# Suffix sums in narrow steps of their own group, shift rows through VectorE and DRAM, operand loads behind them

## The chip, the cores and the metric

One core of one Trainium2 chip. The metric is the device time of one execution in microseconds; a kernel's time is the median of its runs.

## The reference, cut to what matters

```python
x, shape (2, 2048, 256), all float32
xn = layernorm(x)
q, k, v = split(xn @ w_in.T)              # 16 heads of 16
att = (q @ k.T) / 4                       # per head, 2048 x 2048
att = where(causal, att, 0.0)             # a masked score is 0, not -inf
out = softmax(att) @ v                    # so masked keys keep a weight exp(0 - max)
y = x + out @ w_out.T + sigmoid(xr @ W_r.T) * (relu(xk @ W_k.T)**2 @ W_v.T)
# xr, xk: xn mixed with the token before it by mu_r, mu_k
```

Because masked scores are zero, each query needs, besides its causal keys, the plain sum of the values of all later keys: the suffix sum, weighted by exp(-max). And the row maximum of each query has to be known before the exponentials.

## The kernel before

**Token stage** (to about 228 us). Eight chunks of 512 tokens are normalised, projected to q, k, v, run through the feed-forward part and stored in DRAM: q and k as a high and a low part in `parts_d`, v in `vpad_d`.

**Attention stage.** Eight groups of four heads, G = 0 to 7. G is 2i + p, and p (0 or 1) says which half of the double buffers `q_op`, `k_op`, `v_sb`, `v_after` it uses. A group has four units u = 0 to 3 of 512 queries; unit u has 4(u+1) key tiles, so that a group has 40 steps, numbered 0 to 39 here: unit 0 is steps 0 to 3, unit 1 steps 4 to 11, unit 2 steps 12 to 23, unit 3 steps 24 to 39. A step (u, kt) is written out by hand on TensorE: four score matmuls (L1175, one for each head, in two pairs), in between two "pieces" of the row maxima (L330, L337: the scores once more, turned, for VectorE to reduce at L347), then what `between_scores` adds, then `weigh_values` (L1189) of the step two before. The last four key tiles of a unit are on the diagonal and 512, 384, 256 and 128 queries wide; these narrow steps have less score work.

**Row maxima run ahead.** The 80 pieces of a group do not stand in its own steps. From step 17 on (`AHEAD_FROM`, L44) the pieces are those of the next group, 46 of them, and steps 0 to 16 hold the other 34 of the group itself. So piece 0 of the next group, in step 17, is the first thing that reads that group's `q_op` and `k_op`, and TensorE waits for their loads there (L1259 to L1261).

**Shift rows.** When a unit's pieces are reduced, three small VectorE instructions (`max_step`, L349: L355, L359, L362) make its negated maximum in two parts, `shift`, [128 queries, 4 blocks x 8 values]. It is turned by four TensorE transposes into a bank of `ps_s` (`turn_shift`, L1149, L1154), copied by ScalarE (`keep_shift`, L1014, L1019) to `shift_t` [8, 512], and stored by four SP DMAs in rows of `q_op` (`place_shift`, L300, L306), so that the score matmul subtracts it. This stands at `SHIFT_AT` (L55): units 0 and 1 of the next group in steps (3, 3) and (3, 10), unit 2 in (1, 2), unit 3 in (2, 8). Two units are turned in the token stage (`TOKEN_SHIFT_AT`, L52; L744, L667).

**Suffix sums.** GpSimd adds up the values behind each tile (`add_up_after`, L313, L320) in `after`; for each of four quads of tiles TensorE adds two matmuls (`sum_suffix`, L1158: L1164, L1165), and ScalarE copies them to `v_after` (L1011). They are made for the next group, in steps (3, 2), (3, 4), (3, 7), (3, 9) of unit 3 (`SV_AT`, L56); group 0 makes its own in steps (0, 0) to (0, 3). `masked_keys` (L1194) uses them in the second step of the unit behind.

**The ring.** Scores, suffix sums and turned shifts share three banks of `ps_s`; each use waits for ScalarE's reading of the use three before (`wait_for_bank`, L1132), and ScalarE reads in the same order.

**The SP queue** (`group`, L891) is one list of waits and DMAs in order. In a group: wait for the end of the scores of the group before; load the next group's `q_op` and `k_op` (`load_scores`, L275: 12 DMAs of 256 KB); store the normalised output of unit 3 of the group before (`keep_normed`, L879, L884: 4 DMAs, behind a wait for VectorE's L1091); `place_shift` of unit 2; load the next values (L311, 1 MB); the outputs of units 0 and 1; `place_shift` of unit 3; the output of unit 2; `place_shift` of the next group's units 0 and 1. TensorE waits for a unit's shift rows at its first step (L1252).

Of the kernel before, what the change touches and what calls it, by code (L numbers as in the profile page):

```python
# [22 lines left out]
GH = 4  # L23
# [87 lines left out]
def score_uses(first, last):  # L111

    uses = []
    for u in range(NCH):
        for kt in range(key_tiles(u)):
            uses += [("scores", (KT0[u] + kt) * GH + at) for at in range(GH // 2)]
            if first and (u, kt) in FIRST_SV_AT:
                uses.append(("own suffix", FIRST_SV_AT[u, kt]))
            if (u, kt) in SV_AT and not last:
                uses.append(("suffix", SV_AT[u, kt]))  # L120
            if (u, kt) in SHIFT_AT and not (u == NCH - 1 and last):
                uses.append(("shift", SHIFT_AT[u, kt]))
# [72 lines left out]
class Operands:  # L195
# [3 lines left out]
    def __init__(self, nc, ctx, parts_d, vpad_d):  # L199
# [10 lines left out]
        self.after = sb("after", [P, NT, GH, HD])  # L210
# [8 lines left out]
        self.shift_t = sb("shift_t", [SHIFT_PARTS * GH, 2, CH])  # L219
# [12 lines left out]
        self.shift_turned, self.shift_t_ready = sem("shift_turned"), sem("shift_t_ready")  # L232
        self.shift_loaded = [sem("shift_loaded0"), sem("shift_loaded1")]
        self.SHIFTS = SHIFT_PARTS * 2 * 16
        self.parts_in = parts_d.rearrange("r (z b) (cc g e j d) t -> r z (b cc) g e d j t", b=B, cc=CC, g=2, e=2, j=GH // 2)
        self.v_in = vpad_d.rearrange("(i g) p t f -> i g p t f", g=2)

    def set_constants(self, pool):
# [4 lines left out]
        pool.memset(self.after[:, NT - 1], 0.0).then_inc(self.consts_set, 1)  # L243
# [69 lines left out]
    def add_up_after(self, pool, p, n, loads):  # L313
# [3 lines left out]
        for j in range(NT - 2, -1, -1):  # L317
            if j < NT - 2:
                pool.wait_ge(self.after_ready, n * (NT - 1) + NT - 2 - j)
            pool.tensor_tensor(self.after[:, j], self.after[:, j + 1], values[:, j + 1, :, 0:HD], ALU.add).then_inc(self.after_ready, 1)  # L320
# [28 lines left out]
    def max_step(self, dve, k, u, n, reduced):  # L349
# [27 lines left out]
def stage_tokens(nc, block, x, w_in_t, w_r_t, w_k_t, w_v_t, w_out_t, mu_rk,  # L377
                 parts_d, vpad_d, ffn_d, ident, w_out_sb, consts_ready, ops, stores):

    with ExitStack() as ctx:  # L380
# [259 lines left out]
        def _(act):  # L640
# [23 lines left out]
            def keep_shift(u):  # L664

                act.wait_ge(ops.shift_turned, u + 1)
                act.copy(ops.shift_t[:, u], ps_m[0:SHIFT_PARTS * GH, 0]).then_inc(ops.shift_t_ready, 1)  # L667

            def batch(b, last):
                for c in range(NCH):  # L670
# [6 lines left out]
                    if (n, 0) in TOKEN_SHIFT_AT:  # L677
                        keep_shift(TOKEN_SHIFT_AT[n, 0])
# [10 lines left out]
                    if (n, 6) in TOKEN_SHIFT_AT:  # L689
                        keep_shift(TOKEN_SHIFT_AT[n, 6])  # L690
# [14 lines left out]
        def _(pe):  # L705
# [31 lines left out]
            piece_behind_turn = {pieces_beside_tokens(*at).stop: u for at, u in TOKEN_SHIFT_AT.items()}  # L737

            def turn_shift(u, pieces_before):

                pe.wait_ge(ops.shift_ready, u + 1)
                pe.wait_ge(ops.piece_reduced, pieces_before + MRING)
                for s in range(SUB):
                    last = pe.transpose(ps_m[0:SHIFT_PARTS * GH, 0, s * P:(s + 1) * P],  # L744
                                        ops.shift[:, u, s].rearrange("p r h -> p (r h)"), ident[:])
# [573 lines left out]
```

## Time and profile before

| | us |
|---|---|
| median of 3 runs (lowest, highest) | 1128.43 (1125.78, 1129.91) |
| the profiled execution's own time | 1134.35 |
| its span | 1132.6 |
| TensorE busy | 1080.0 (95%) |
| VectorE busy | 842.5 (74%) |
| ScalarE busy | 713.4 (63%) |
| GpSimd busy | 385.8 (34%) |
| mean granted clock of TensorE | 0.983 |

The profile is one execution, recorded by the hardware. A busy TensorE is one that has some matmul under way, which isn't a TensorE at its peak: matmuls are pipelined, and pairs of them run side by side. SPq is the SP engine's DMA queue; the time beside a DMA there is that of its issue, not of its transfer. "Issue" as a releaser is a wait for nothing that the profile shows. The clock column gives 1.00 for 2.4 GHz and 0.50 for 1.2 GHz.

### The profile page before, as it was taken

The page shows a single profiled execution, that of the slowest core. Times are in us where ns is not written, and L with a number is a line of the kernel's source. Part 1 is how long each engine was busy: PE and PEld are TensorE (multiplying, and loading weights), DVE is VectorE, ACT ScalarE, POOL GpSimd, SP SyncE. Part 2 cuts the span into 40 slices and gives each one's busy share as a digit, 9 for nine tenths or more (in the row PEclk, how much of TensorE's full clock was granted, in tenths as well). Part 3 has the DMA queues.
Part 4 walks back from the last instruction along what each step waited for, and adds up shares of the span by engine and source line. Part 5 has one row for each costly group of instructions (what it writes and reads, how often), then busy time and mean ns, then how long its engine had stood idle before and what let it go on. Part 6 is the DMA issues. An engine that isn't in the chain of part 4 may idle for free.

```text
span 1132.6 us, 21906 instructions
## 1 busy us (share of the span) xinstructions
PE 1080.0 (95%) x8192; PEld 542.6 (48%) x8192; DVE 842.5 (74%) x1153; ACT 713.4 (63%) x1519; POOL 385.8 (34%) x945
## 2 busy tenths in 40 slices
PE   5999998999999999999989999999999989999998
PEld 3665554544444444444435444444444434444445
DVE  5567787678879787987867878878887878789213
ACT  2433333267776677777757776777777657767672
POOL 3211121354414341444224424442532433244301
PEclk9999999999999899999969999999999989999999
DMA  3585744392019000900280019002800460002033
GB/s 127 174 271 177 214 149 149 131 117 62 2 20 122 30 3 17 124 31 7 37 119 11 6 22 140 8 7 38 124 6 6 58 104 7 6 2 86 25 98 117
DMA packets 53390, 83.61 MB, mean 74 GB/s; under 512 B 6308, under 2 KB 36260, under 8 KB 49572
## 3 DMA queue, kind: packets, MB, share of 16 engines
q1 hardware_dynamic: 52132, 78.01, 32.9%
q0 software_dynamic: 1152, 4.19, 1.2%
q8 instruction: 65, 1.06, 0.4%
q14 instruction: 41, 0.34, 0.1%
HBM read 43.78 MB, written 33.55 MB: 68 GB/s over the span
## 4 chain that ended last, share of the span: by engine, by line
PE 75%; DVE 13%; ACT 4%; issue 4%; DMA 2%; POOL 0%; SPq 0%; ACTq 0%; DVEq 0%; POOLq 0%
PE ps_o L1189 22%; PE ps_s L1175 21%; DVE part_max L347 10%; PE ps_m L330 7%; PE ps_vr L733 4%; ACT probs L1039 4%; PE ps_qk L724 4%; PE ps_m L1220 3%; PE ps_o L1200 2%; PE ps_m L337 2%; PE ps_xt L782 2%; PE ps_qk L733 2%; PE ps_s L1164 2%; DMA x_in<-x 1%; PE ps_pieces L330 1%
## 5 line engine op out<-in xcount | busy, mean ns | idle before, releaser
L1039 ACT ACTIVATE probs<-ps_s 128x512 f32<-128x512 f32 (+3 forms) x1280 | 599.6, 536 | 249.6 <-PE ps_s L1175 241.5
L347 DVE TENSOR_REDUCE part_max<-ps_m 128x2 f32<-128x1024 f32 (+2 forms) x594 | 616.6, 1059 | 152.7 <-PE ps_m L330 115.1
L1175 PE MATMUL ps_s<-q_op,k_op 50*128 50x512 f32 (+3 forms) x1280 | 447.9, 429 | 10.0 <-ACT probs L1039 5.2
L330 PE MATMUL ps_m<-k_op,q_op 48*128 48x512 f32 (+3 forms) x1188 | 355.3, 419 | 16.6 <-DVE part_max L347 9.4
L1175 PEld LDWEIGHTS ps_s<-q_op,k_op 50*128 50x128 f32 x1280 | 210.7, 188 | 313.1 <-ACT probs L1039 214.2
L984 POOL TENSOR_SCALAR_AFFINE_SELECT probs<-probs 128x128 f32<-128x128 f32 x512 | 145.0, 292 | 485.7 <-ACT probs L1039 477.2
L1189 PE MATMUL ps_o<-probs,v_sb 128*32 128x512 f32 (+3 forms) x2560 | 307.9, 551 | 2.2 <-issue 2.2
L330 PEld LDWEIGHTS ps_m<-k_op,q_op 48*128 48x128 f32 x1188 | 169.3, 189 | 43.8 <-DVE part_max L347 33.8
L950 POOL TENSOR_TENSOR diag_weight<-ident,masked_weight 128x256 f32<-128x256 f32 x256 | 150.5, 623 | 40.7 <-ACT masked_weight L1005 40.7
L337 PE MATMUL ps_m<-mask,pick 64*128 64x64 bf16 (+1 forms) x932 | 96.5, 210 | 0.0
L1189 PEld LDWEIGHTS ps_o<-probs,v_sb 128*32 128x32 f32 x2560 | 51.1, 108 | 76.7 <-issue 38.1
L347 DVE TENSOR_REDUCE part_max<-ps_pieces 128x2 f32<-128x1024 f32 (+3 forms) x46 | 46.5, 1011 | 35.2 <-PE ps_pieces L337 18.4
L724 PE MATMUL ps_qk<-xn_t,w_in_sb 128*128 128x512 f32 x128 | 63.2, 624 | 1.9 <-issue 1.4
L656 ACT ACTIVATE parts<-ps_qk 128x512 fp32r<-128x512 f32 x32 | 19.1, 597 | 71.2 <-PE ps_qk L724 71.2
L516 POOL TENSOR_TENSOR k_act<-k_act 128x1024 f32<-128x1024 f32 x8 | 15.3, 1909 | 122.4 <-ACT k_act L688 122.4
L337 PEld LDWEIGHTS ps_m<-mask,pick 64*128 64x128 bf16 x932 | 46.6, 97 | 9.9 <-issue 2.5
L320 POOL TENSOR_TENSOR after<-after,v_sb 128x64 f32<-128x64 f32 x120 | 39.5, 329 | 8.8
L521 POOL TENSOR_TENSOR ffn<-ffn,x_in 128x512 f32<-128x512 f32 x16 | 21.4, 1345 | 51.4 <-DVE ffn L589 51.4
L724 PEld LDWEIGHTS ps_qk<-xn_t,w_in_sb 128*128 128x128 f32 x128 | 23.5, 196 | 25.2 <-issue 24.1
L1200 PE MATMUL ps_o<-diag_weight,v_after 128*32 128x128 f32 x1024 | 35.2, 279 | 0.0
L1220 PE MATMUL ps_m<-w_out_sb,attn_t 128*128 128x256 f32 x128 | 33.3, 397 | 0.0
L1200 PEld LDWEIGHTS ps_o<-diag_weight,v_after 128*32 128x32 f32 x1024 | 26.7, 111 | 11.6 <-POOL diag_weight L950 8.0
(81 smaller groups left out, 715.9 us busy)
## 6 DMA issues: line engine op xcount, KB each, us to landing
parts_d<-parts SPq DMA_DIRECT2D x32, 512.0 KB, 4.7
q_op<-parts_d SPq DMA_DIRECT2D x42, 256.0 KB, 13.9
k_op<-parts_d SPq DMA_DIRECT2D x42, 256.0 KB, 16.2
vpad_d<-v_pad SPq DMA_DIRECT2D x32, 256.0 KB, 3.3
v_sb<-vpad_d SPq DMA_DIRECT2D x8, 1024.0 KB, 12.4
x_in<-x SPq DMA_DIRECT2D x8, 512.0 KB, 5.2
ffn_d<-ffn SPq DMA_DIRECT2D x8, 512.0 KB, 3.2
attn_t<-normed SPq DMA_DIRECT2D x128, 32.0 KB, 2.0
```

The source lines that it names most:

```text
L330: last = pe.matmul(ps_m[:, f % ring * 2 + e, 0:width], self.q_op[rows, p, j, q0:q0 + P], self.k_op[rows, p, j, pc * CH:pc * CH + width], s ...
L337: last = pe.matmul(ps_m[:, f % ring * 2 + e, s * P + k * HALF:width], self.pick16[half, k], self.mask16[half, k, k * HALF:P], start=False, ...
L347: dve.tensor_reduce(both, ps_m[:, bank:bank + 2, 0:width], AX_X, ALU.max).then_inc(self.piece_reduced, 1)
L724: last = pe.matmul(ps_qk[:, j % 2], w_in_sb[:, cc, j * P:(j + 1) * P], xn_t[:, cc, 1:CH + 1], start=(cc == 0), stop=(cc == CC - 1))
L733: last = pe.matmul(psum[:, s], lhs[:, cc, t * P:(t + 1) * P], weights[:, cc], start=(cc == 0), stop=(cc == CC - 1))
L950: pool.tensor_tensor(diag_weight[:, u % 2, some], ident[:].unsqueeze(1).broadcast_to([P, GH * SUB // DIAGS, P]), masked_weight[:, u, some] ...
L984: pool.affine_select(out=blk, in_=blk, compare_op=ALU.is_ge, fill=0.0, base=0, pattern=[[1, P]], channel_multiplier=-1).then_inc(probs_mas ...
L1039: act.activation(probs[:, slot % PRING, 0:width], ps_s[:, bank_of("scores", slot, first, last), 0:width], ACT.Exp).then_inc(probs_ready, 1)
L1175: pe.matmul(ps_s[:, bank_of("scores", slot, first, last), 0:CH - q0], k_op[rows, p, h % 2, kt * P:(kt + 1) * P], q_op[rows, p, h % 2, u * ...
L1189: last = pe.matmul(ps_o[h * HW:(h + 1) * HW, q0:CH], v_sb[:, p, kt, h * HW:(h + 1) * HW], probs[:, ((KT0[u] + kt) * GH + at) % PRING, 0:CH ...
L1200: last = pe.matmul(ps_o[h * HW:(h + 1) * HW, s * P:(s + 1) * P], v_after[:, p, u * SUB + s, h * HW:(h + 1) * HW], diag_weight[:, u % 2, h ...
L1220: last = pe.matmul(ps_m[:, k % MBANKS, 0:C], attn_t[:, b * CC + cc, c * CH + t * P:c * CH + (t + 1) * P], w_out_sb[:, cc], start=(cc == 0) ...
```

## The change

The suffix sums of a group are made in that group itself, in its steps (0, 2), (0, 3), (1, 6) and (2, 10), and `after` becomes a double buffer, so that GpSimd no longer waits for its readers. The shift is no longer turned on TensorE: a fourth `max_step` on VectorE transposes [128, 32] in blocks of 32 x 32, SP stores the result in a DRAM tensor `shift_d` by four DMAs, waits until they have landed, and loads the rows of `q_op` from there by four DMAs. In the SP queue, `load_scores` stands behind `keep_normed` of unit 3 and `place_shift` of unit 2. The bank order of `ps_s` runs on through all groups.

```diff
-TOKEN_SHIFT_AT = {(6, 0): 0, (6, 6): 1}
-SHIFT_AT = {(3, 3): 0, (3, 10): 1, (1, 2): 2, (2, 8): 3}
-SV_AT = {(3, 2): 0, (3, 4): 1, (3, 7): 2, (3, 9): 3}
-FIRST_SV_AT = {(0, 0): 0, (0, 1): 1, (0, 2): 2, (0, 3): 3}
-MAX_STEPS = 3
+WEIGHT_AT = {(3, 3): 0, (3, 10): 1, (1, 2): 2, (2, 8): 3}
+SV_AT = {(0, 2): 0, (0, 3): 1, (1, 6): 2, (2, 10): 3}
+MAX_STEPS = 4
...
-def bank_of(what, which, first, last):
+def bank_of(what, which, G):
-    return (score_uses(first, last).index((what, which)) + 2 * first) % SRING
+    return (G * len(score_uses()) + score_uses().index((what, which))) % SRING
...
-        self.after = sb("after", [P, NT, GH, HD])
+        self.after = sb("after", [P, 2, NT, GH, HD])
-        self.shift_t = sb("shift_t", [SHIFT_PARTS * GH, 2, CH])
+        self.shift_t = sb("shift_t", [P, 2, HW])
+        self.shift_d = nc.dram_tensor("shift_d", [2, SHIFT_PARTS, 2, GH // 2, CH], F32, kind="Internal").ap()
...
     def place_shift(self, sp, p, u, n):
         sp.wait_ge(self.shift_t_ready, n + 1)
+        sp.wait_ge(self.shift_loaded[u % 2], (n // 2 + 1) * self.SHIFTS)
+        by_block = self.shift_d[u % 2].rearrange("r e j (s b w) -> b s (r e j) w", s=SUB, w=HW)
+        for b in range(P // HW):
+            sp.dma_start(by_block[b], self.shift_t[b * HW:(b + 1) * HW, u % 2]).then_inc(self.shift_stored, 16)
+        sp.wait_ge(self.shift_stored, (n + 1) * (P // HW) * 16)
         for part in range(SHIFT_PARTS):
             for e in range(2):
-                row, at = e * HALF + ROWS + part, part * GH + e * 2
+                row = e * HALF + ROWS + part
                 sp.dma_start(self.q_op[row:row + 1, p, :, u * CH:(u + 1) * CH].bitcast(F32),
-                             self.shift_t[at:at + 2, u % 2]).then_inc(self.shift_loaded[u % 2], 16)
+                             self.shift_d[u % 2, part, e].unsqueeze(0)).then_inc(self.shift_loaded[u % 2], 16)
...
+        if k == 3:
+            dve.wait_ge(self.shift_ready, n + 1)
+            if n >= 2:
+                dve.wait_ge(self.shift_stored, (n - 1) * (P // HW) * 16)
+            dve.transpose(self.shift_t[:, u % 2], self.shift[:, u].rearrange("p s r h -> p (s r h)")).then_inc(self.shift_t_ready, 1)
...
             def group(i, p, first=False, last=False):          # SP
-                if not last:
-                    if not first:
-                        sp.wait_ge(scores_ready, (i * 2 + p) * SLOTS)
-                    ops.load_scores(sp, i + p, 1 - p)
                 if not first:
                     keep_normed(i - 1 + p, 1 - p, NCH - 1)
                 ops.place_shift(sp, p, 2, unit_of(i, p, 2))
                 if not last:
+                    if not first:
+                        sp.wait_ge(scores_ready, (i * 2 + p) * SLOTS)
+                    ops.load_scores(sp, i + p, 1 - p)
                     sp.wait_ge(masked_done, unit_of(i, p, 0) + 1)
                     sp.wait_ge(probs_used, weighed_to(unit_of(i, p, 0)))
                     ops.load_values(sp, i + p, 1 - p)
...
                     if u == 2 and not last:                    # GpSimd
-                        pool.wait_ge(v_after_ready, G * 4 + 4)
                         ops.add_up_after(pool, 1 - p, G + 1, i + 1 + p)
...
             def masked_keys(p, u, G):                          # TensorE
                 pe.wait_ge(diag_ready, (G * NCH + u + 1) * DIAGS)
-                pe.wait_ge(v_after_ready, G * 4 + 4)
+                pe.wait_ge(v_after_ready, G * 4 + u + 1)
...
-                if (u, kt) in SV_AT and not last:
-                    wait_for_bank("suffix", SV_AT[u, kt], i, p, first, last)
-                    sum_suffix(1 - p, SV_AT[u, kt], G + 1, bank_of("suffix", SV_AT[u, kt], first, last))
-                if (u, kt) in SHIFT_AT and not (nxt and last):
-                    v = SHIFT_AT[u, kt]
-                    wait_for_bank("shift", v, i, p, first, last)
-                    turn_shift(v, unit_of(i, p, v + nxt), bank_of("shift", v, first, last))
+                if (u, kt) in SV_AT:
+                    wait_for_bank("suffix", SV_AT[u, kt], i, p, first)
+                    sum_suffix(p, SV_AT[u, kt], G, bank_of("suffix", SV_AT[u, kt], G))
```

Both `turn_shift` and both `keep_shift` functions, of the token and of the attention stage, go with their calls and their bank uses; `weight` (L1002) stays at the places in `WEIGHT_AT`.

## Rows read from the trace of the kernel before

**Rows 1.** The page: busy time, share of the span and instructions.

```profile
PE 1080.0 (95%) x8192; PEld 542.6 (48%) x8192; DVE 842.5 (74%) x1153; ACT 713.4 (63%) x1519; POOL 385.8 (34%) x945
```

**Rows 2.** TensorE's instructions in time, group 5: start us, us, engine, line.

```profile
785.10 0.50 PE L1175 MATMUL ps_s<-q_op,k_op 50*128 50x512 f32 x1
...
829.54 0.32 PE L330 MATMUL ps_m<-k_op,q_op 48*128 48x128 f32 x1
...
837.54 0.50 PE L1175 MATMUL ps_s<-q_op,k_op 50*128 50x512 f32 x1
...
840.72 0.44 PE L1175 MATMUL ps_s<-q_op,k_op 50*128 50x384 f32 x1
...
871.53 0.50 PE L1175 MATMUL ps_s<-q_op,k_op 50*128 50x512 f32 x1
...
874.20 0.50 PE L1175 MATMUL ps_s<-q_op,k_op 50*128 50x512 f32 x1
...
877.72 0.49 PE L1175 MATMUL ps_s<-q_op,k_op 50*128 50x512 f32 x1
```

**Rows 3.** The SP queue in time, groups 5 and 6: start us, us of issue.

```profile
784.42 0.31 SPq L280 DMA_DIRECT2D q_op<-parts_d  x1
...
789.44 0.42 SPq L282 DMA_DIRECT2D k_op<-parts_d  x1
799.62 3.75 SPq L884 DMA_DIRECT2D attn_t<-normed  x4
803.42 2.46 SPq L306 DMA_DIRECT2D q_op<-shift_t  x4
...
907.79 2.48 SPq L884 DMA_DIRECT2D attn_t<-normed  x4
```

**Rows 4.** DMA issues in 789.4 to 789.9 us: KB, us to landing.

```profile
k_op<-parts_d SPq DMA_DIRECT2D x1, 256.0 KB, 24.7
```

**Rows 5.** DMA issues in 832.3 to 832.6 us.

```profile
attn_t<-normed SPq DMA_DIRECT2D x2, 32.0 KB, 1.9
```

**Rows 6.** Stretches: us, busy of the engines, clock, DMA share, GB/s.

```profile
676.10:688.00 11.90, 11.35 (x130) 5.83 (x126) 11.68 (x17) 8.53 (x21) 7.17 (x22) 1.00 1.04 126
...
829.50:893.30 63.80, 62.93 (x526) 30.17 (x522) 48.99 (x61) 46.69 (x104) 18.44 (x48) 1.00 0.03 6
```

**Rows 7.** The same view around the longest idle stretches of TensorE.

```profile
573.00:576.00 3.00, 0.20 (x2) 0.20 (x2) 0.23 (x1) 0.43 (x1) 0.00 (x0) 0.95 1.07 117
576.00:597.00 21.00, 21.00 (x106) 9.31 (x106) 13.48 (x15) 11.55 (x24) 3.35 (x12) 0.52 0.68 114
...
903.00:910.00 7.00, 4.00 (x57) 1.99 (x53) 4.69 (x6) 3.80 (x7) 4.43 (x8) 1.00 1.04 117
910.00:917.00 7.00, 6.83 (x35) 2.84 (x35) 4.03 (x4) 4.14 (x8) 0.00 (x0) 0.51 1.03 118
```

**Rows 8.** The SP queue, the same store in groups 1, 3, 4 and 7.

```profile
352.60 2.47 SPq L884 DMA_DIRECT2D attn_t<-normed  x4
...
573.26 2.46 SPq L884 DMA_DIRECT2D attn_t<-normed  x4
...
690.60 2.45 SPq L884 DMA_DIRECT2D attn_t<-normed  x4
...
1021.23 2.45 SPq L884 DMA_DIRECT2D attn_t<-normed  x4
```

**Rows 9.** Groups of instructions: count, busy us, mean ns, idle before.

```profile
L320 POOL TENSOR_TENSOR after<-after,v_sb 128x64 f32<-128x64 f32 x120 | 39.5, 329 | 8.8
...
L1091 DVE STREAM_TRANSPOSE normed<-turned 128x512 f32<-128x512 f32 x32 | 22.4, 701 | 0.0
...
L362 DVE SCALAR_TENSOR_TENSOR shift<-row_max,shift 128x16 f32<-128x16 f32 x32 | 5.9, 185 | 0.3
```

**Rows 10.** TensorE in time in the token stage, around its two turned shifts.

```profile
175.40 0.44 PE L330 MATMUL ps_pieces<-k_op,q_op 48*128 48x384 f32 x2 [1.14 <-ACT shift_t L667]
...
191.50 0.49 PE L330 MATMUL ps_pieces<-k_op,q_op 48*128 48x512 f32 x2 [1.57 <-ACT shift_t L667]
```

More of the change, by code:

```diff
@@ L108, in pieces_at, with score_uses @@
     return SPREAD[u, kt, half], KT0[u] + kt >= AHEAD_FROM
-def score_uses(first, last):
+def score_uses():
     uses = []
@@ L735, in two_tiles @@
                 return last
[L737 to L745, printed above, removed]
-                last.then_inc(ops.shift_turned, 1)
             def batch(b, last_batch):
@@ L1039, in group @@
                             act.activation(probs[:, slot % PRING, 0:width],
-                                           ps_s[:, bank_of("scores", slot, first, last), 0:width], ACT.Exp).then_inc(probs_ready, 1)
+                                           ps_s[:, bank_of("scores", slot, i * 2 + p), 0:width], ACT.Exp).then_inc(probs_ready, 1)
                             if h != GH // 2 - 1:
                                 continue
-                            if first and (u, kt) in FIRST_SV_AT:
-                                keep_suffix(0, FIRST_SV_AT[u, kt], FIRST_SV_AT[u, kt],
-                                            bank_of("own suffix", FIRST_SV_AT[u, kt], first, last))
-                            if (u, kt) in SV_AT and not last:
-                                keep_suffix(1 - p, SV_AT[u, kt], (G + 1) * 4 + SV_AT[u, kt],
-                                            bank_of("suffix", SV_AT[u, kt], first, last))
-                            if (u, kt) in SHIFT_AT and not (nxt and last):
-                                v = SHIFT_AT[u, kt]
-                                weight(unit_of(i, p, v + nxt), v)
-                                keep_shift(v, unit_of(i, p, v + nxt), (G + (nxt > 0)) * (NCH // 2) + v // 2,
-                                           bank_of("shift", v, first, last))
+                            if (u, kt) in SV_AT:
+                                keep_suffix(p, SV_AT[u, kt], G * 4 + SV_AT[u, kt], bank_of("suffix", SV_AT[u, kt], G))
+                            if (u, kt) in WEIGHT_AT and not (nxt and last):
+                                weight(unit_of(i, p, WEIGHT_AT[u, kt] + nxt), WEIGHT_AT[u, kt])
                         if kt == LAG - 1 and not (first and u == 0):
@@ L1131, in _, with wait_for_bank @@
         def _(pe):
-            def wait_for_bank(what, which, i, p, first, last):
-                uses = score_uses(first, last)
+            def wait_for_bank(what, which, i, p, first):
+                uses = score_uses()
                 G = i * 2 + p
@@ L1141, in wait_for_bank @@
                     pe.wait_ge(probs_ready, G * SLOTS + uses[at][1] + 1 + SRING)
-                elif uses[at][0] == "own suffix":
-                    pe.wait_ge(v_after_ready, uses[at][1] + 1)
-                elif uses[at][0] == "suffix":
-                    pe.wait_ge(v_after_ready, (G + 1) * 4 + uses[at][1] + 1)
-                else:
-                    pe.wait_ge(shift_t_ready, unit_of(i, p, uses[at][1] + (NCH if uses[at][1] < 2 else 0)) + 1)
-            def turn_shift(u, n, bank):
-                pe.wait_ge(shift_ready, n + 1)
-                for s in range(SUB):
-                    last = pe.transpose(ps_s[0:SHIFT_PARTS * GH, bank, s * P:(s + 1) * P],
-                                        shift[:, u, s].rearrange("p r h -> p (r h)"), ident[:])
-                last.then_inc(shift_turned, 1)
+                else:
+                    pe.wait_ge(v_after_ready, G * 4 + uses[at][1] + 1)
             def sum_suffix(p, quad, n, bank):
@@ L1164, in sum_suffix @@
                 pe.matmul(ps_s[:, bank, 0:width], keys_after[:], values, start=True, stop=False)
-                pe.matmul(ps_s[:, bank, 0:width], ones[:], after[:, tiles].rearrange("p s h d -> p (s h d)"),
+                pe.matmul(ps_s[:, bank, 0:width], ones[:], after[:, p, tiles].rearrange("p s h d -> p (s h d)"),
                           start=False, stop=True).then_inc(suffix_ready, 1)
@@ L1173, in score_tile @@
                 q0 = first_query(u, kt)
-                wait_for_bank("scores", slot, i, p, first, last)
-                pe.matmul(ps_s[:, bank_of("scores", slot, first, last), 0:CH - q0], k_op[rows, p, h % 2, kt * P:(kt + 1) * P],
+                wait_for_bank("scores", slot, i, p, first)
+                pe.matmul(ps_s[:, bank_of("scores", slot, i * 2 + p), 0:CH - q0], k_op[rows, p, h % 2, kt * P:(kt + 1) * P],
                           q_op[rows, p, h % 2, u * CH + q0:(u + 1) * CH], start=True, stop=True).then_inc(scores_ready, 1)
@@ L1233, in between_scores @@
                     output_tile(OUT_AT[u, kt])
[L1234 to L1243 removed]
+                if (u, kt) in SV_AT:
+                    wait_for_bank("suffix", SV_AT[u, kt], i, p, first)
+                    sum_suffix(p, SV_AT[u, kt], G, bank_of("suffix", SV_AT[u, kt], G))
             def group(i, p, first=False, last=False):
```

38 lines of the change are left out of this document (6 added, 32 removed).

## The prediction

> **What bounds the kernel now.** I read the page first: TensorE is busy 95% of the span [rows 1]. The chain of waits and the SP queue's own view come next, since this change touches TensorE's list, VectorE's list and the order of the SP queue. From step 12 on a group is TensorE's: in the stretch from step 17 to the end of group 5 it is busy 62.93 of 63.80 us with VectorE at 48.99 (the second of [rows 6]), and a plain step of unit 3 takes 874.20 - 871.53 = 2.67 us, start to start [rows 2]. Steps 0 to 4 are VectorE's: 11.68 busy of 11.90 us, TensorE 11.35 (the first of [rows 6]). Then the loads: the twelve DMAs of the next group's scores are issued from 784.42 on, 0.7 us before the group's first matmul at 785.10 [rows 2, 3], and the last, issued at 789.44, lands 24.7 us later, at 814.1 [rows 3, 4]. That is 29.7 us for 3 MB, with the DMA engines full (share 1.04 in the first stretch of [rows 6]). The first reader, piece 0 of the next group, starts at 829.54 [rows 2]. So the loads have 15.4 us of slack. That slack is what the change spends.
>
> **The start of the loads.** New order in the SP queue: output of unit 3, shift of unit 2, then the loads. The output waits for VectorE and is issued 799.62 - 785.10 = 14.5 us into the group. Behind it: four issues, 2.5 us (3.75 here); four stores of the shift, of which the last is issued 1.85 us after the first (three quarters of 2.46 for four issues [rows 3]) and lands some 1.9 us later [rows 5]; four loads of the rows, 2.5 us; with 0.4 us between them 9.2 us in all. The loads start at 14.5 + 9.2 = 23.7 us of the group instead of -0.7, and land 30 us later, at 53.7.
>
> The output itself comes later by x: two suffix sums (0.85 each on TensorE, below) and VectorE's fourth step stand ahead of it in steps 2 and 3. Nothing of it shows if VectorE hides it (TensorE is idle 0.55 of 11.90 us there), 1.9 if nothing hides it. I take x = 0.9, the middle, since the rows show both engines nearly full.
>
> **When they are wanted.** Step 17 starts 829.54 - 785.10 = 44.4 us into the group. It loses one turned shift (-0.5), gains x and y, the suffix sum in (1, 6), which costs 0 to 0.85; I take 0.5. That is 44.4 - 0.5 + 0.9 + 0.5 = 45.3. The loads land at 53.7 + 0.9 = 54.6. **TensorE stands still for 9.3 us in step 17 of groups 1 to 6.** Groups 1 to 6 alone: group 7 has no loads, and in group 0 SP waits for no output, only for the maximum of unit 2 in step 2, so its loads start at about 9 + 6.6 us (an estimate: the time of four steps, then stores, wait and loads), land at 46 and cost 0 to 1 us.
>
> **What the stall costs behind it.** The trace has two such gaps, both shorter. TensorE is busy 0.20 us from 573 to 576, and the granted clock is 0.52 for the 21 us behind it, which is 1.2 GHz. In 903 to 910 it is idle 3.0 us, and the clock is 0.51 for the next 7 us [rows 7]. From output to output those groups take 690.60 - 573.26 = 117.3 and 1021.23 - 907.79 = 113.4 us, against 907.79 - 799.62 = 108.2 for group 5 [rows 3, 8]. Less the gap (2.8 and 3.0) the low clock costs 6.3 and 2.2 us. I take C = 3.8 for each stall, nearer to the middle than to an end, as nothing says which it will be.
>
> The Trainium skill (TensorE: Matmul & The Clock Gate, HAM oscillation) tells of a matmul kernel that waits for DMA once in each iteration and runs the start of every iteration at the low clock. By it C is paid in all six groups. The sum above takes C six times as well; only if a gap left the clock alone would it be less.
>
> **What the change saves.** A turned shift costs 840.72 - 837.54 = 3.18 us for its step, against 2.67: 0.5 us, four in a group. A suffix sum in unit 3 costs 877.72 - 874.20 = 3.52, so 0.85 [rows 2]. Of the four in unit 3 I count 3.05: three at 0.85 and 0.5 for the one in (3, 2), where ScalarE's copy of the unit before comes between the scores and would hold the step up anyway. The same sums come back in narrow steps: x, y and 0.85 in (2, 10), where [rows 6] shows TensorE full. So narrow steps save little, because TensorE's own work for a sum is the same and only VectorE's steps 0 to 4 could hide it. ScalarE's copies go at no gain of their own: it was ahead.
>
> Added on VectorE: 32 transposes of 128 x 32. The trace has 128 x 512 at 0.70 us as the upper end, and the neighbour L362 on 128 x 16 at 0.19 as the lower [rows 9]; I take 0.2, as these short ones are all start-up. In steps 16, 22 and 30 TensorE covers it, which would cost 0.2 to 0.7 each uncovered; in step 2 it is in x. GpSimd's sums wait for the values, which now land at about 59 instead of 33 us of the group; its masks for step 20 then queue up to 5 us behind (15 sums of 0.33 [rows 9]), and their reader stands two steps later, so I cost it at 0, at most 2 us a group. The shift rows are wanted at 8 to 17 us after SP gets to them and take 7: cost 0, with up to 2 in unit 3, where they queue behind the values.
>
> **The sum.** The part behind step 17 was 108.2 - 44.4 = 63.8 us. It becomes 63.8 - 1.5 (three turned shifts) - 3.05 + 0.85 = 60.1. A group: 54.6 + 60.1 + 3.8 = 118.5. Six of them: 711.0, against 1021.23 - 352.60 = 668.6 before [rows 8]: +42.4. (In those 668.6 stand the two stalls above and smaller ones, all ahead of step 17 while the loads run. They are paid for already now: whatever is lost ahead of step 17 is taken out of the wait there.) Group 0: four turned shifts and the later sums, -2.0 - 3.05 with its own four sums only moved, +0.5 of wait: -4.5. Group 7: it had no sums and two turned shifts: +0.9 + 0.5 + 0.85 - 1.0 = +1.3. Token stage: two turned shifts with the gaps of 1.14 and 1.57 us behind them [rows 10] and 0.5 each: between 0 and -4; -3. Sum: 42.4 - 4.5 + 1.3 - 3.0 = +36.2 on the profiled execution's 1134.35, that is 1170.5. The median of the runs shown is 1128.43, 5.9 lower; stalls ahead of step 17 that vary from run to run would be absorbed in the new kernel, so I take off only 2.5 of it: **1168 us**, 3.5% slower.
>
> **The rivals.**
>
> *The loads land in time (faster).* Point of decision: they must take 45.3 - 24.6 = 20.7 us or less where [rows 3, 4] show 29.7. For it: behind the shift they run beside other traffic, and no row shows them at another place. Against it: the engines' share is already 1.04 with nothing else in the queue but 128 KB of outputs. Then a group is worth 2.0 + 3.05 - 0.9 - 0.5 - 0.85 = 2.8 less, six groups -17, with group 0, 7 and the token stage -23: about 1110 from the profiled execution's time. The Trainium skill (DMA: Bandwidth & Descriptors, Measured) gives 6.15 us for 1 MB spread over 128 partitions, some 18 us for 3 MB as an estimate, and by it this rival would hold. These rows go to 16 partitions each, the trace has 29.7 us, and the measurement decides. Chance 0.08.
>
> *The loads are late by some 4 us (no change).* If they take 25 us, six stalls of 4 us with little low clock give back what the steps saved: about 1128. Chance 0.04.
>
> *The low clock lasts.* The stall is three times as long as the ones of the trace. If each costs the 6.3 us of group 3 or a little more, six times 2.5 to 4 is added: 1183 to 1192. Chance 0.15.
>
> *The change doesn't do what it says.* The first reader of the loads would have to stand later than step 17, so that no wait arises. `AHEAD_FROM` and L1259 are untouched; I see no way, and fold it into the first rival.
>
> The forecast itself has 0.73.
>
> **The range.** Its bounds are 29.7 or 31 us for the loads (-2 to +6 over six groups), C from 2.2 to 6.3 (-10 to +15), y (-3 to +2; x cancels in the stall but not in the arrival: -5 to +6), GpSimd and the shift of unit 3 (up to +10), token stage (-1 to +3), the distance to the median (-3.5 to +2.5). Together I give 1148 to 1189, which leaves out the first two rivals and the far end of the third. A measurement of this kernel tells 0.5% from no change. Faster by more: 0.08. Within: 0.04. Slower: 0.88.
>
> **What the new profile would show.** Right: in groups 1 to 6 a wait of about 9 us of TensorE at L330's weight load, released by a DMA into `q_op` or `k_op`, once a group; DMA-filled slices in the middle of a group; the clock at 0.5 behind each wait; plain steps of unit 3 at 2.67 with no 3.5 among them; six groups of 117 to 120 us; the first stalls for which nothing is shown gone from the sum. Wrong: loads that land within 21 us; a wait at step 17 under 5 us; an unmoved clock behind it (then -20 us); or shift rows that come late for unit 2 or 3, which would show as waits on `q_op<-shift_d` at L1175.

## The result, and the profile after

| | before | after |
|---|---|---|
| median (lowest, highest), 4 runs each on one chip, us | 1129.17 (1125.78, 1132.36) | 1181.68 (1178.22, 1184.88) |
| ratio, 95% interval | | 1.0465 (1.0415 to 1.0514) |
| the profiled execution's own time, its span, us | 1134.35, 1132.6 | 1184.88, 1182.8 |
| mean granted clock of TensorE | 0.983 | 0.942 |

The change makes the kernel 4.7% slower. I measured each group from its first score matmul to that of the next group, in us. These lengths are used all the way down:

| kernel | group 0 | groups 1 to 6 (sum) | group 7 to the end |
|---|---|---|---|
| before | 110.4 | 113.0, 107.7, 117.3, 109.0, 108.2, 113.5 (668.6) | 125.9 |
| after | 114.6 | 118.1, 118.5, 120.3, 119.5, 118.4, 120.3 (715.1) | 127.4 |

So the groups 1 to 6 take 46.5 us more, group 0 4.2 more, group 7 1.5 more; the first group starts 2.0 us earlier (225.64 against 227.65). Together 50.2, the difference of the spans.

The page of the kernel after: busy times, then the slices of TensorE, its clock and the DMA engines, then two groups of instructions (busy us, mean ns, idle before and its releaser):

```profile
PE 1091.6 (92%) x8064; PEld 550.5 (47%) x8064; DVE 847.0 (72%) x1185; ACT 699.6 (59%) x1487; POOL 386.0 (33%) x945
...
PE   5999999999999699969997999799969996999998
...
PEclk9999999879999799979996999699979996999999
DMA  4575644391006400640064006500550055002033
...
L330 PEld LDWEIGHTS ps_m<-k_op,q_op 48*128 48x128 f32 x1188 | 176.8, 196 | 88.5 <-issue 45.6
...
L320 POOL TENSOR_TENSOR after<-after,v_sb 128x64 f32<-128x64 f32 x120 | 39.4, 328 | 136.6 <-DMA v_sb<-vpad_d 127.9
```

Read the slices together. TensorE has a dent once in each of the groups 1 to 6, the dent follows on the fullest DMA slices, and the clock is down in the same slice. In slices 8 and 9 the clock is down without a dent: that is group 0. TensorE ran 128 fewer matmuls than in [rows 1] and was busy 11.6 us longer: part of its work ran at the low clock. GpSimd waited 127.9 us for the values, seven times, against 8.8 us of all idle time before [rows 9], and nobody was held up by it here.

The SP queue of group 5, whose first matmul starts at 816.66 (start, us of issue):

```profile
832.61 2.47 SPq L864 DMA_DIRECT2D attn_t<-normed  x4
835.18 2.60 SPq L301 DMA_DIRECT2D shift_d<-shift_t  x4
838.93 2.34 SPq L306 DMA_DIRECT2D q_op<-shift_d  x4
841.31 0.40 SPq L275 DMA_DIRECT2D q_op<-parts_d  x1
...
846.42 0.42 SPq L277 DMA_DIRECT2D k_op<-parts_d  x1
```

And the landing of the last of these loads (KB, us to landing):

```profile
k_op<-parts_d SPq DMA_DIRECT2D x1, 256.0 KB, 24.9
```

It answers to [rows 3, 4]: the output stands at +15.95 us of the group instead of +14.5, the loads start at +24.65 instead of -0.7, and the last lands at 846.42 + 24.9 = 871.3, or +54.7. They took 30.0 us, as before (29.7). TensorE at that time:

```profile
862.03 0.49 PE L1125 MATMUL ps_s<-q_op,k_op 50*128 50x512 f32 x1
...
871.45 0.47 PE L330 MATMUL ps_m<-k_op,q_op 48*128 48x128 f32 x2 [8.93 <-issue]
...
873.59 1.93 PE L1139 MATMUL ps_o<-probs,v_sb 128*32 128x512 f32 x8
```

Step 17 begins at +45.4, and piece 0 follows 9.4 us later, 0.1 us after the landing (9.0 to 9.6 us in the six groups, 9.3 in the mean). The idle time is put down to "issue", although what ended it is a load. The chain that ended last gives the load its place (start, us, what):

```profile
845.96 23.83 DMA q_op<-parts_d
869.79 1.67 issue
871.45 0.47 PE ps_m L330 x2
```

In the chain the load has its whole way of 23.83 us, where TensorE lost 9: on the page's chain that makes a share of 14% for DMA, though the six waits are 5% of the span. Last, the stretches around the wait (busy of PE, PEld, DVE, ACT, POOL; clock; DMA share; GB/s):

```profile
862.00:864.50 2.50, 0.52 (x5) 0.18 (x1) 1.64 (x5) 0.62 (x2) 0.00 (x0) 1.00 1.00 111
864.50:871.50 7.00, 0.05 (x2) 0.08 (x2) 0.00 (x0) 0.00 (x0) 0.00 (x0) 0.50 0.98 159
871.50:881.60 10.10, 10.10 (x62) 5.55 (x62) 4.29 (x6) 4.67 (x9) 4.78 (x15) 0.50 0.23 71
881.60:935.00 53.40, 52.37 (x436) 24.35 (x435) 43.09 (x53) 39.25 (x88) 18.41 (x48) 1.00 0.02 5
```

The clock falls to 1.2 GHz while TensorE waits and stays there for the first 10.1 us of work. Step 18 takes 4.45 us and step 19 3.02, where a plain one takes 2.67.

### The profile page after: what moved, and what is told of

Same layout as the page of the kernel before. It is cut to its first block, busy times and chain, and to the rows that moved or that the text cites. A ratio compares the mean times of both kernels' runs of the same rounds, so it can differ in the third digit from the quotient of the medians.

```text
span 1182.8 us, 21770 instructions
## 1 busy us (share of the span) xinstructions
PE 1091.6 (92%) x8064; PEld 550.5 (47%) x8064; DVE 847.0 (72%) x1185; ACT 699.6 (59%) x1487; POOL 386.0 (33%) x945
## 3 DMA queue, kind: packets, MB, share of 16 engines
q8 instruction: 63, 1.03, 0.4%
## 4 chain that ended last, share of the span: by engine, by line
PE 65%; DMA 14%; DVE 11%; issue 4%; ACT 3%; SPq 2%; POOL 0%; ACTq 0%; DVEq 0%; POOLq 0%
PE ps_o L1139 19%; PE ps_s L1125 17%; DMA q_op<-parts_d 12%; DVE part_max L347 7%; PE ps_m L330 7%; PE ps_vr L729 4%; ACT probs L1009 3%; PE ps_qk L720 3%; PE ps_m L1170 3%; PE ps_xt L763 2%; PE ps_m L337 2%; PE ps_qk L729 2%; PE ps_o L1150 2%; PE ps_s L1114 1%; DMA x_in<-x 1%
## 5 line engine op out<-in xcount | busy, mean ns | idle before, releaser
L1125 PE MATMUL ps_s<-q_op,k_op 50*128 50x512 f32 (+3 forms) x1280 | 457.7, 442 | 9.1 <-ACT probs L1009 5.2
L1125 PEld LDWEIGHTS ps_s<-q_op,k_op 50*128 50x128 f32 x1280 | 218.3, 194 | 320.5 <-ACT probs L1009 225.7
L1139 PE MATMUL ps_o<-probs,v_sb 128*32 128x512 f32 (+3 forms) x2560 | 315.8, 567 | 0.0
L330 PEld LDWEIGHTS ps_m<-k_op,q_op 48*128 48x128 f32 x1188 | 176.8, 196 | 88.5 <-issue 45.6
L337 PE MATMUL ps_m<-mask,pick 64*128 64x64 bf16 (+1 forms) x932 | 104.2, 223 | 0.0
L320 POOL TENSOR_TENSOR after<-after,v_sb 128x64 f32<-128x64 f32 x120 | 39.4, 328 | 136.6 <-DMA v_sb<-vpad_d 127.9
L337 PEld LDWEIGHTS ps_m<-mask,pick 64*128 64x128 bf16 x932 | 51.1, 104 | 16.0 <-issue 3.2
L720 PEld LDWEIGHTS ps_qk<-xn_t,w_in_sb 128*128 128x128 f32 x128 | 23.4, 195 | 25.4 <-issue 23.6
L1150 PEld LDWEIGHTS ps_o<-diag_weight,v_after 128*32 128x32 f32 x1024 | 26.7, 111 | 11.6 <-POOL diag_weight L928 6.2
```

The lines of the kernel that those rows point to most:

```text
L330: last = pe.matmul(ps_m[:, f % ring * 2 + e, 0:width], self.q_op[rows, p, j, q0:q0 + P], self.k_op[rows, p, j, pc * CH:pc * CH + width], s ...
L337: last = pe.matmul(ps_m[:, f % ring * 2 + e, s * P + k * HALF:width], self.pick16[half, k], self.mask16[half, k, k * HALF:P], start=False, ...
L720: last = pe.matmul(ps_qk[:, j % 2], w_in_sb[:, cc, j * P:(j + 1) * P], xn_t[:, cc, 1:CH + 1], start=(cc == 0), stop=(cc == CC - 1))
L1125: pe.matmul(ps_s[:, bank_of("scores", slot, i * 2 + p), 0:CH - q0], k_op[rows, p, h % 2, kt * P:(kt + 1) * P], q_op[rows, p, h % 2, u * CH ...
L1139: last = pe.matmul(ps_o[h * HW:(h + 1) * HW, q0:CH], v_sb[:, p, kt, h * HW:(h + 1) * HW], probs[:, ((KT0[u] + kt) * GH + at) % PRING, 0:CH ...
L1150: last = pe.matmul(ps_o[h * HW:(h + 1) * HW, s * P:(s + 1) * P], v_after[:, p, u * SUB + s, h * HW:(h + 1) * HW], diag_weight[:, u % 2, h ...
```

## The experiments

**Theory.** The loads start behind the output and the shift's two trips and land after step 17 has begun. Groups 1 to 6 each pay some 9.4 us of wait and some 4 us of low clock. **Rivals.** The shift's way through DRAM, its added transfers, or the suffix sums in narrow steps cost the time. And for group 0, which has no such wait of this length and yet is 4.2 us longer, something else must be found. Where nothing else is said, a kernel is the one after with the edit shown.

### Only the loads put back in front

```diff
             def group(i, p, first=False, last=False):          # SP
+                if not last:
+                    if not first:
+                        sp.wait_ge(scores_ready, (i * 2 + p) * SLOTS)
+                    ops.load_scores(sp, i + p, 1 - p)
                 if not first:
                     keep_normed(i - 1 + p, 1 - p, NCH - 1)
                 ops.place_shift(sp, p, 2, unit_of(i, p, 2))
                 if not last:
-                    if not first:
-                        sp.wait_ge(scores_ready, (i * 2 + p) * SLOTS)
-                    ops.load_scores(sp, i + p, 1 - p)
```

> The changed kernel with the twelve score loads put back in front of the output of unit 3 and the shift of unit 2. Theory (the time is lost at step 17, waiting for loads that start 24.7 us into the group): the wait of 9.3 us and the low clock behind it go, a group is 105.5 us (the clean steps of the changed kernel) plus a wait in step 12, because the shift rows of unit 2 now stand behind the loads twice: stored at about 30 us of the group, loaded at about 34.5 where step 12 starts at 31.5, so some 3 us; with stalls ahead of step 17 as in the kernel before (0 to 23 us in all) 1115 to 1140 us, ratio to before 0.99 to 1.01. Rival (the trip of the shift rows through DRAM is what costs, wherever the loads stand): stays above 1165 us, with waits for shift rows in every unit.

Measured: 1129.14 us, ratio 0.9972 (0.9943 to 1.0001). Groups 1 to 6 take 664.3. All the loss is gone, so what the change adds elsewhere doesn't cost it. But no gain is left either, and the rows of unit 2 now come late in step 12 (waited for: us in total, times, longest):

```profile
PEld ps_s L1126 <- DMA q_op<-shift_d: 11.6, 4, 3.2
...
PE ps_s L1126 <- DMA q_op<-shift_d: 8.8, 4, 2.5
```

With the loads in front of them, the shift's two trips run while the DMA engines are full: in groups 1 to 6 the last load of the rows is issued 11 to 12 us after the last of the stores, against 3.6 us in the kernel after. I expected such a wait of some 3 us in each group; it came in four of seven, and the other three lose their time elsewhere (last section).

### Shift, loads, output

```diff
             def group(i, p, first=False, last=False):          # SP
-                if not first:
-                    keep_normed(i - 1 + p, 1 - p, NCH - 1)
                 ops.place_shift(sp, p, 2, unit_of(i, p, 2))
                 if not last:
                     if not first:
                         sp.wait_ge(scores_ready, (i * 2 + p) * SLOTS)
                     ops.load_scores(sp, i + p, 1 - p)
+                if not first:
+                    keep_normed(i - 1 + p, 1 - p, NCH - 1)
```

> The changed kernel with the SP queue in the order shift of unit 2, score loads, output of unit 3. The shift is ready 6.9 us into the group and takes 6.2 us on SP, so the loads start at 13.3 and land at 43.4, ahead of step 17 at 45.4. Theory: no wait at step 17, a group of 105.5 us plus what the loads' own stalls cost (0 to 23 us over six groups): 1099 to 1124 us, ratio 0.975 to 0.995, faster than both. Rival (the low clock comes from the narrow steps or the DRAM trip and not from the wait): the clock still falls in each group, over 1150 us.

Measured: 1102.18 us, ratio 0.9713 (0.9664 to 0.9761). Groups 1 to 6 take 633.7, five of them 105.5 to 105.8. In group 5, which starts at 762.68:

```profile
773.53 2.33 SPq L306 DMA_DIRECT2D q_op<-shift_d  x4
775.91 0.40 SPq L275 DMA_DIRECT2D q_op<-parts_d  x1
...
781.48 2.47 SPq L864 DMA_DIRECT2D attn_t<-normed  x4
```

The loads start at +13.2 and have landed at +43.1; step 17 begins at +45.4, and nothing waits. The order of three entries in one queue is worth some 80 us; by the profiles it is 81.4 in groups 1 to 6. The time is in the expected range, the ratio a little below it. This kernel also gives the full price of a late group: (715.1 - 633.7) / 6 = 13.57 us, less 9.33 of wait in the mean, leaves 4.2 for what comes behind it. Group 0 stayed at 114.7, so its loss has another cause.

### The first reader three steps later

```diff
-AHEAD_FROM = 17
+AHEAD_FROM = 20
```

> The changed kernel with AHEAD_FROM 20 instead of 17: the loads stay where they are, their first reader moves three steps of 2.67 us later, to 53.4 us of the group, against 54.7 for the landing. Theory: a wait of 1.3 us in step 20 instead of 9.3 in step 17, too short for the clock: groups of 107 us, 1105 to 1120 us in all. Rival (the DMA traffic in the middle of the group slows the steps themselves): no better than 1165 us.

Measured: 1150.15 us, ratio 1.0145 (1.0083 to 1.0208): 31 us less than after, and at least 30 above what I expected. Groups 1 to 6 take 688.6. In step 20 the wait is 0 to 2.4 us (1.3 expected). A larger wait stands in step 22, which takes 3.22 us in the kernel after and 4.6 to 7.8 here: it is behind GpSimd. Group 5, GpSimd and then TensorE:

```profile
848.68 5.88 POOL L320 TENSOR_TENSOR after<-after,v_sb 128x64 f32<-128x64 f32 x15 [18.92 <-DMA v_sb<-vpad_d]
854.51 2.98 POOL L961 TENSOR_SCALAR_AFFINE_SELECT probs<-probs 128x128 f32<-128x128 f32 x12
```

```profile
855.60 1.06 PE L1139 MATMUL ps_o<-probs,v_sb 128*32 128x512 f32 x4 [1.51 <-POOL probs L961]
```

GpSimd stands before its suffix sums until the values, the last of the loads, have landed; twelve masks of unit 2's diagonal queue up behind, and their reader waits for them. In the kernel after, the wait in step 17 held TensorE back by more than that, so nothing showed.

### The same, with GpSimd's sums a unit later

```diff
-AHEAD_FROM = 17
+AHEAD_FROM = 20
...
-                    if u == 2 and not last:                    # GpSimd
+                    if u == 3 and not last:
                         ops.add_up_after(pool, 1 - p, G + 1, i + 1 + p)
```

> The kernel with AHEAD_FROM 20 (1150 us, with waits of 2.4 to 4.6 us in step 22 that nobody foresaw), and GpSimd's adding up of the values moved from the start of unit 2 to the start of unit 3 in its list. Theory (GpSimd waits for the values, which land behind the scores at 59 us of the group, and its masks for steps 20 and 21 are queued behind the sums): the wait in step 22 goes, groups of 106 to 108 us, 1100 to 1112 us in all. Rival (the DMA traffic at that time or the narrow steps themselves are slow): step 22 keeps its wait, 1145 us or more.

Measured: 1126.31 us, ratio 0.995 (0.9918 to 0.9982), groups 1 to 6 657.1. Step 22 takes 3.23 us in every group instead of 4.6 to 7.8: GpSimd was the cause. The size is missed by some 14 us. The profiled execution took 1115.26 us, 11 less than the median, so its groups show less than the usual loss. What is left in it against the 633.7 of the order above: waits of up to 2.4 us in step 20, and steps 2 to 8, which are longer with the pieces at other places, with low clock in steps 6 to 8 of three groups and behind the wait in two.

### The kernel before, with only the SP queue's new order

```diff
             def group(i, p, first=False, last=False):          # SP, before.py
-                if not last:
-                    if not first:
-                        sp.wait_ge(scores_ready, (i * 2 + p) * SLOTS)
-                    ops.load_scores(sp, i + p, 1 - p)
                 if not first:
                     keep_normed(i - 1 + p, 1 - p, NCH - 1)
                 ops.place_shift(sp, p, 2, unit_of(i, p, 2))
+                if not last:
+                    if not first:
+                        sp.wait_ge(scores_ready, (i * 2 + p) * SLOTS)
+                    ops.load_scores(sp, i + p, 1 - p)
```

> The kernel before with one part of the change alone: the loads behind the output of unit 3 and the shift of unit 2. They start 14.5 + 2.7 + 2.6 = 19.8 us into the group and land at 49.8; step 17 stands at 44.4. Theory: a wait of 5.4 us and 2 to 4 us of low clock in six groups, a group of 116.3 us, less the stalls ahead of step 17, which the wait absorbs: 1150 to 1168 us, ratio 1.02 to 1.035. Rival (the order of the loads alone does nothing, the narrow steps and the DRAM trip do it): within 0.5% of before.

Measured: 1183.33 us, ratio 1.0441 (1.0397 to 1.0485). The groups 1 to 6 take 701.6. Without one transpose on VectorE or one sum moved, the reordering alone costs as much as the whole change does. That the totals are so near is chance, since the parts differ. Groups 1 to 6 lose 33.0 us here and 46.5 with the whole change: the loads start at +19.7 instead of +24.65, and the wait is 4.6 to 5.8 us instead of 9.3. Group 0 loses 13.0 us here and 4.2 there, and it is why the total is above what I expected. It takes 123.4 us against 110.4: its loads stand behind the shift of unit 2, which TensorE turns only in step 6. They start 22.1 us into the group, TensorE waits 5.8 us in step 17, and the clock stays low for 23.9 us.

```profile
248.31 2.39 SPq L306 DMA_DIRECT2D q_op<-shift_t  x4
250.74 0.40 SPq L280 DMA_DIRECT2D q_op<-parts_d  x1
```

### TensorE kept busy in the wait

Nine dummy matmuls (128 x 512, the identity by `w_out_sb`, into a bank of `ps_m` that is overwritten next; the trace lists two rows for each) stand in front of the wait, in group 0 too, which has none. No work is left out.

```diff
                                     if ahead and f == 0:
+                                        pe.wait_ge(ops.piece_reduced, (G + ahead) * PIECES + 1)
+                                        for _ in range(WARM):
+                                            pe.matmul(ps_m[:, 0], ident[:], w_out_sb[:].rearrange("p a c -> p (a c)"),
+                                                      start=True, stop=True)
                                         pe.wait_ge(q_loaded[1 - p], ops.loaded(1 - p, i + 1 + p))
```

> The changed kernel, with nine matmuls of 128 x 512 (0.94 us each at the full clock, 8.5 us, by the projections of the token stage) put ahead of the wait in step 17, written to a bank that piece 0 then overwrites. They do no work; they only fill the 9.3 us of the wait. Theory (13 us lost a group are 9.3 of waiting and the rest of low clock behind it): the wait stays, the clock stays at 2.4 GHz, and six groups win 3 to 5 us each: 1150 to 1165 us. Rival A (all the loss is waiting, the low clock only shows it): same as the changed kernel, 1182. Rival B (nine matmuls more are work more): slower than 1182 by up to 50 us.

Measured: 1159.72 us, ratio 1.0248 (1.0211 to 1.0286). Groups 1 to 6 take 689.1, 25.9 less than after. The loads are as late as they were, and piece 0 starts 8.8 to 9.8 us behind its step; what differs is the clock. Group 5:

```profile
847.61 7.99 PE L1206 MATMUL ps_m<-w_out_sb,ident 128*128 128x512 f32 x18
856.60 0.33 PE L331 MATMUL ps_m<-k_op,q_op 48*128 48x128 f32 x2 [0.99 <-issue]
```

```profile
849.00:858.70 9.70, 8.71 (x39) 3.65 (x37) 1.62 (x3) 1.35 (x3) 0.00 (x0) 1.00 0.90 176
```

The gain is 25.9 / 6 = 4.3 us a wait, but the clock held in five groups only. In group 4, where TensorE idled 1.33 us behind the dummies (1.18 at most in the others), it fell for 6.8 us, and the group took 117.3 us. The other five, at 114.1 to 114.7, are 4.8 us shorter in the mean than in the kernel after. That agrees with the 4.2 from above: with the clock kept, these five groups are 8.7 us longer than without a wait, though piece 0 starts 9.2 us late, so that 0.4 us of a wait is won back and the low clock itself has to cost some 4.7.

### Where the suffix sums stand

Three kernels, each on the order "shift, loads, output". In the first the sums of steps (0, 2) and (0, 3) go to the two steps ahead of them:

```diff
-SV_AT = {(0, 2): 0, (0, 3): 1, (1, 6): 2, (2, 10): 3}
+SV_AT = {(0, 0): 0, (0, 1): 1, (1, 6): 2, (2, 10): 3}
```

> The kernel with the SP order shift, loads, output (1102 us), and the first two suffix sums in steps (0, 0) and (0, 1) instead of (0, 2) and (0, 3). Theory (in group 0 the sums of the kernel before filled the gaps of TensorE in the first two steps of the attention stage, and without them the clock falls for 24 us and costs some 8 us): group 0 keeps its clock and is 8 us shorter, other groups within 1 us of before, 1090 to 1097 us. Rival (the clock falls in group 0 for another reason, such as the hand-over of the stages): no difference beyond 2 us.

Measured: 1098.68 us, ratio 0.972 (0.9688 to 0.9752). Group 0 takes 105.5 instead of 114.7, and the clock keeps its level there; each of the groups 1 to 6 pays 0.75 us more (638.2 in all), which puts the total 1.7 us above the expected range and, by its ratio, not clear of the 0.9713 of the order above. In the second they stand in wide steps:

```diff
-SV_AT = {(0, 2): 0, (0, 3): 1, (1, 6): 2, (2, 10): 3}
+SV_AT = {(1, 0): 0, (2, 0): 1, (3, 0): 2, (3, 4): 3}
```

> The same kernel with the four suffix sums of a group in wide steps: (1, 0), (2, 0), (3, 0), (3, 4). Theory (a sum is 0.85 us of TensorE wherever it stands, and the narrow steps hid only a fourth of it: 2.6 us for four against 3.4): 0.8 us more a group, +3 to +9 us over 1102. Rival (narrow steps hide the sums altogether): +25 us. A third way: group 0 without its sums in the narrow steps may lose or win some us by the clock.

Measured: 1098.78 us, ratio 0.9716 (0.9681 to 0.9751). Groups 1 to 6 take 633.6, that is 105.6 each with sums in wide steps, and 105.5 in the clean groups with narrow ones. The placement that names the change is worth 0.1 us a group at most. I expected 0.8, and 3 to 9 us more in all; neither came, and by their ratios, 0.9716 and 0.9713, the two kernels are equal. The third takes the early places in group 0 alone:

```diff
+SV_FIRST = {(0, 0): 0, (0, 1): 1, (1, 6): 2, (2, 10): 3}
+def sums_at(G):
+    return SV_FIRST if G == 0 else SV_AT
```

> The kernel with the SP order shift, loads, output, and the first two suffix sums in steps (0, 0) and (0, 1) in group 0 alone; the other groups have them in (0, 2) and (0, 3). Theory (group 0 needs them to bridge its first gaps, the others are 0.75 us shorter with the narrow steps): group 0 is 105.5 us with its clock kept, the others 105.5 as well, 1092 to 1096 us, ratio 0.965 to 0.972. Rival (the early sums only happened to keep the clock in that one profile): group 0 has a low clock in half of the runs, no better than 1098 us.

Measured: **1093.67 us, ratio 0.9664 (0.9634 to 0.9694)**, groups 0 to 6 at 105.4 to 106.0. The mean clock is 0.997 to 1.000 in all six runs, so the kept clock is no accident of one profile. It is the best of all kernels here, 88 us below the one after and 3.4% below the one before:

```profile
PE 1052.5 (97%) x8064; PEld 530.6 (49%) x8064; DVE 844.6 (78%) x1185; ACT 696.4 (64%) x1487; POOL 385.9 (35%) x945
...
PEclk9999999999999999999999999999999999999999
```

## Why the forecast was right, and where it was wrong

**The mechanism holds.** Sign, place and cause are as forecast, and the range of 1148 to 1189 holds the 1181.68. The order of the SP queue alone gives the kernel before a wait in step 17 of groups 0 to 6 and 33.0 of the 46.5 us of groups 1 to 6, and undoing it alone in the kernel after removes the loss. The clock fell at each of the six waits, so that C is paid six times as the sum has it. Against the profiled spans, +36.2 was forecast and +50.2 came, 14.0 us off.

**The start of the loads and step 17, right by two errors that cancel, which is luck.** They were to start at +24.6 and started at +24.65, but the chain behind the output took 8.7 us where I had 9.2, and x was 1.45 us, not 0.9: VectorE doesn't hide the two sums in steps 2 and 3 (3.16 and 2.92 us, where the kernel before takes 2.58 and 1.88). Landing +54.7 (54.6), step 17 +45.4 (45.3), stall 9.4 (9.3). As forecast, x cancels in the stall and not in the time of arrival.

**C, 3.8 forecast, 4.2 measured.** That is in the prediction's own terms, where the wait is paid in full; the kernel with the busy wait puts the low clock alone at some 4.7. The two stretches that I had to bound it from (6.3 and 2.2 us) held it; I took a value near the middle for want of a reason and was 0.4 short, 2.5 us over six groups. Group 5 alone is 118.4 - 105.5 - 9.4 = 3.5 us longer than without the wait, for 10.1 us of work at the low clock. The Trainium skill (TensorE: Matmul & The Clock Gate, HAM oscillation) takes half of the throttled time as the penalty. That would be 5.05 us; the measurement decides, and it is 3.5, or 3.9 against group 5 of the kernel with the busy wait (118.4 - 114.4), whose piece 0 starts at the same +54.8. No other engine sets these steps: in the 10.10 us TensorE is busy throughout, VectorE 4.29 and ScalarE 4.67. The step itself isn't twice as long: step 18 takes 4.45 us at the low clock against 2.67, and one of its score matmuls 0.79 against 0.50. Which part of a matmul doesn't follow the clock isn't shown. The rival "the low clock lasts" (1183 to 1192) had the price at 6.3 or more a stall and falls, although the time came near it and the clock was low for 13.7 to 20.5 us at a wait, the part inside the wait among them.

**What the steps save, right.** The plain steps of unit 3 are at 2.67 with no 3.5 among them. The sum in step 10 cost 0.35 (0.5 forecast), the sum in (2, 10) cost 1.0 (0.85), VectorE's transposes 0.20 each. For groups 1 to 6 all this comes to 715.1 against 711.0.

**Group 0 is the term that failed.** I put it at -4.5, it was +4.2: 8.7 of the 14.0 us (4.1 are of groups 1 to 6). I had costed its own four sums as "only moved". They had filled TensorE's gaps at the start of the attention stage. The kernel after, then the kernel before, the same stretch from 2.6 us ahead of the group's first matmul on:

```profile
223.00:229.60 6.60, 4.48 (x26) 2.87 (x25) 4.31 (x6) 2.23 (x5) 5.39 (x8) 1.00 0.24 80
229.60:253.50 23.90, 23.90 (x136) 12.07 (x136) 13.53 (x16) 11.75 (x28) 10.48 (x27) 0.50 0.58 71
```

```profile
225.00:231.60 6.60, 5.04 (x28) 3.23 (x26) 3.28 (x4) 2.22 (x6) 5.38 (x8) 1.00 0.34 97
231.60:255.50 23.90, 23.33 (x193) 11.55 (x196) 20.50 (x24) 17.70 (x43) 12.19 (x34) 1.00 1.03 116
```

With 4.48 of 6.60 us busy ahead of it the clock fell for 23.9 us, with 5.04 it held. In these 23.9 us TensorE ran 136 matmuls instead of 193. Sums put back into steps (0, 0) and (0, 1) bring group 0 to 105.4, against 105.9 by my sum without a low clock. All eleven profiles agree: the clock fell at the start of group 0 in the seven without sums in its first two steps and held in the four with them. How long it stays low isn't fixed: 6.8 us in three of the seven, 23.9 in two. One of the three is the kernel with the busy wait, whose code is that of the kernel after up to step 17. So the 8.7 us are the profiled execution's, and another may lose less.

I could have known. I worked with the two falls behind gaps of 3 us. The trace of the kernel before has a third, in group 1, behind no gap above 1.28 us, and I left it out:

```profile
360.00:368.00 8.00, 6.62 (x50) 2.50 (x46) 6.65 (x8) 4.40 (x12) 3.24 (x12) 0.97 0.98 140
368.00:378.00 10.00, 10.00 (x82) 5.00 (x74) 5.58 (x6) 4.16 (x10) 7.59 (x19) 0.51 0.21 78
```

**The rest.** The token stage saved 2.0 of the 3.0 us. In the six other kernels with the same token stage the first group starts between 222.7 and 225.9 us, so this term is known to some 3 us only. Group 7 lost 1.5 (1.3). The 2.5 us that I took off for the distance of the profiled execution to the median was 3.2 in the kernel after (1184.88 - 1181.68).

**GpSimd, costed at 0.** Right for this kernel, and only because the wait in step 17 stood in front of it. It was the bound as soon as that wait was moved to step 20: step 22 became 1.3 to 4.6 us longer. I had written the cost as 0 to 2 us a group without saying that the stall is its cover.

**The other rivals.** The loads didn't land in time (30.0 us, not 20.7), and they weren't late by 4 but by 9.4. That the narrow steps or the way through DRAM cost the time is refuted by the kernel with the order shift, loads, output, which keeps both and is 2.9% faster than before. The kernel before, with its turned shifts and its sums in unit 3, wasn't run with that order, so how much of the 3.4% of the best kernel is the order's isn't known.

## What to carry to other kernels

A transfer that is "hidden" has a slack in microseconds. Before its place in a queue is changed, add up what now stands in front of it, waits included, and set that against the slack (15.4 us here, 25.4 spent). A stall at a full TensorE costs more than its length, here 4.2 us on 9.3; and small work in the gaps of a stage that starts up can be worth more than its own time, since it keeps the clock. If a later place for a reader doesn't bring what the wait cost, look for the next late arrival behind it before the theory is dropped.

## What the runs showed of the hardware that was not expected

- The clock fell in group 0 with no gap of TensorE above 1.10 us in the stretch ahead of it, and the low stretch (23.9 us) was longer than any around the waits of 9.0 to 9.6 us (13.7 to 20.5). In the two kernels with the first reader in step 20 it fell seven times in steps 6 to 8 with no gap above 0.29 us in the 10 us ahead. The Trainium skill (TensorE: Matmul & The Clock Gate, A second HAM failure mode) tells of a matmul kernel whose many small idle times between groups of matmuls made the clock swing. This trace agrees in that short gaps were enough, with 4.48 busy of 6.60 us.
- Nine dummy matmuls (7.99 us) held the clock at 1.00 through a wait for a DMA in five of six groups; in the sixth it fell, with 1.33 us left open behind them against 1.18 at most in the others.
- A wait of TensorE that a load ended is listed as "issue" (8.93 us), as in five of the six groups; the wait of group 4 is put down to the DMA. The landing time of the last load and the chain show what it was.
- With the loads issued ahead of everything, groups 1 to 6 take 664.3, with the same loads 14 us later 633.7, and no wait for them in either. The stalls that the kernel before has ahead of step 17 stay in the first and are missing in the second, though the DMA engines are full in both. The late shift rows of step 12 explain four groups of the first (0, 2, 3 and 4); in 1, 5 and 6 steps 5 to 8 are up to 4 us longer. These stalls have no releaser in the profile. One candidate shows in the trace: the queue that the page calls "instruction". In the attention stages of the kernel before and of the one with the loads in front, TensorE has seven waits of 0.9 to 3.0 us on "issue", all while the loads run, and each ends 3.2 to 3.8 us after a packet of 16 KB of that queue has started. An eighth, of 1.03 us in the kernel before with the new order, does the same. Around the 3.00 us of group 3:

```profile
q1 hardware_dynamic: 140, 0.77, 97.7%
q8 instruction: 1, 0.02, 1.6%
```

Other such packets pass without a stall, also while the loads run (groups 2 and 5 of the kernel before), and no run tests it: that TensorE waited there for its instructions, behind the loads, is not shown.
